# Scan: later weighing in quads of one block; convolution and token norm as one stage

## What is computed

```python
# 1. x = x + L1_conv(_gn(x)), then the layer norm of each token over its 128 channels
h = conv_depthwise_3x3(x) + dw_b
h = prune(relu(bn1(h)), 4.0)          # a channel whose maximum is under 4.0 becomes zero
h = conv_1x1(h) + pw_b
h = prune(relu(bn2(h)), 0.001)
t = to_tokens(x + h)
t = t + L2_attn(_ln_t(t), ...)        # _ln_t: (v - mean) / sqrt(var + eps) of each token

# 2. L3_attn, on 8 heads of 16 channels
iq, ik, iv = (softmax((x @ w).reshape(B, T, H, 16) / 0.1) for w in (wq, wk, wv))
a = einsum(iq, ik)                    # T x T per head
y[r, c] = a[r, c] * (y[r-1, c-1] + 1) # the scan, along each diagonal
p = causal_softmax((y + position) / 0.1)
o = einsum(p, iv)
```

## Time and profile before

| | |
|---|---|
| median of the runs | 3854.08 us (3847.75 to 3857.21) |
| the profiled execution, time / span | 3845.83 / 3844.1 us |
| TensorE clock granted, mean of the span | 0.909 of full speed |
| busy, share of the span: PE, PEld, DVE, ACT, POOL | 86%, 54%, 80%, 49%, 28% |
| convolution, from the first clearing of `pad` | 956 to 1062.4 us |
| token norm n2 | 1063.2 to 1103.6 us |
| scan of the first group: one-block quads, two-block quads | 1854 to 2156, 2156 to 2630 us |
| scan of the second group | from 2754 us, alike |

### The profile page before, as it was taken

How to read it: one execution, slowest core, us unless ns; L and a number is a source line. 1 busy time by engine, 2 the same in 40 slices (tenths; PEclk the granted TensorE clock), 3 DMA queues, 4 the chain that set the end, 5 groups by cost and what they waited for, 6 DMA issues and landing times. The chain is left out here.

```text
span 3844.1 us, 131192 instructions
## 1 busy us (share of the span) xinstructions
PE 3294.1 (86%) x53977; PEld 2075.7 (54%) x53977; DVE 3087.6 (80%) x7677; ACT 1888.9 (49%) x4422; POOL 1077.9 (28%) x1932
## 2 busy tenths in 40 slices
PE   5999999997768849966799999997689999999329
PEld 1323223332357636643577888775377788877214
DVE  7878788883868856668789999997778999997677
ACT  1666566666245524444566655553466655554200
POOL 1000111100003455520455434331165533332000
PEclk7999999999889969975799999997599999999659
DMA  7023333200010122240000000000000000000128
GB/s 151 18 41 57 57 57 57 54 8 10 0 67 27 35 57 77 78 150 18 8 10 13 12 4 9 9 6 5 7 10 10 10 10 10 10 4 6 52 95 301
DMA packets 104351, 155.92 MB, mean 41 GB/s; under 512 B 17060, under 2 KB 65193, under 8 KB 103728
## 3 DMA queue, kind: packets, MB, share of 16 engines
q1 hardware_dynamic: 90064, 121.41, 12.6%
q0 software_dynamic: 12544, 21.93, 2.1%
q10 hardware_dynamic: 1152, 4.19, 0.3%
HBM read 103.21 MB, written 45.30 MB: 39 GB/s over the span
## 5 line engine op out<-in xcount | busy, mean ns | idle before, releaser
L2095 ACT ACTIVATE s_E<-s_Y,s_M 128x9 f32<-128x9 f32 (+38 forms) x2048 | 656.6, 393 | 626.1 <-DVE s_M L2008 624.2
L369 DVE TENSOR_REDUCE half_max<-shared 128x1 f32<-128x512 f32 x1024 | 644.1, 684 | 85.7 <-PE shared L290 83.9
L1909 PE MATMUL g_x<-s_ik,s_iqm 128*32 128x1 f32 (+63 forms) x16384 | 675.2, 280 | 25.8 <-DVE g_o L1991 11.6
L492 ACT ACTIVATE E<-sc 128x1024 f32<-128x1024 f32 x512 | 497.0, 1021 | 276.1 <-PE sc L304 276.0
L2003 DVE SCALAR_TENSOR_TENSOR s_Y<-s_Y,g_x 128x9 f32<-128x9 f32 (+38 forms) x2048 | 578.2, 282 | 46.6 <-PE g_x L1909 1.2
L1921 PE MATMUL g_p<-mats,s_E 128*128 128x128 f32 x3072 | 449.9, 284 | 40.6 <-ACT s_E L2095 36.8
L1909 PEld LDWEIGHTS g_x<-s_ik,s_iqm 128*32 128x32 f32 x16384 | 393.7, 116 | 152.7 <-issue 77.1
L1921 PEld LDWEIGHTS g_p<-mats,s_E 128*128 128x128 f32 x3072 | 340.3, 144 | 107.1 <-ACT s_E L2095 62.6
L290 PE MATMUL shared<-ks,qs 96*128 96x512 bf16 x1024 | 373.6, 402 | 20.4 <-DVE half_max L369 16.7
L2008 DVE TENSOR_REDUCE s_M<-s_Y 128x4 f32<-128x8 f32 (+56 forms) x512 | 351.1, 686 | 0.2
L2019 DVE TENSOR_TENSOR resid<-g_p,s_W 128x512 f32<-128x512 f32 x384 | 263.6, 686 | 61.8 <-PE g_p L1921 58.1
(11 more groups left out here) (358 smaller groups left out, 5054.4 us busy)
## 6 DMA issues: line engine op xcount, KB each, us to landing
e_spread<-d_gate SPq DMA_DIRECT2D x64, 512.0 KB, 6.0
d_parts<-parts SPq DMA_DIRECT2D x8, 1536.0 KB, 5.9
qs<-d_parts SPq DMA_DIRECT2D x96, 128.0 KB, 7.6
ks<-d_parts SPq DMA_DIRECT2D x96, 128.0 KB, 12.4
me_xg<-d_xs SPq DMA_DIRECT2D x144, 65.0 KB, 1.8
mc_yb<-d_ys SPq DMA_DIRECT2D x8, 1024.0 KB, 5.8
resid<-in_x SPq DMA_DIRECT2D x8, 512.0 KB, 8.1
rden<-d_den POOLq DMA_DIRECT2D x16, 256.0 KB
```

What stands on the lines that cost most here:

```text
L369: dve.tensor_reduce(half_max[n // SETS % 2][:, idx // 2, idx % 2:idx % 2 + 1], bank("bm", n)[:, :], AX_X, ALU.max).then_inc(max_done, 1)
L492: act.activation(E[:, G % 2, h, :], sc[n % 2][:, :], ACT.Exp, scale=0.25).then_inc(exp_done, 1)
L1909: mm = pe.matmul(x_ps[u % 3][32 * b:32 * (b + 1), rho % 2, 0:n + 1], iqm[n // WINDOW % 2][:, b, x0:x0 + D, :], s.ik[:, b, rho, 0:n + 1], s ...
L2095: act.activation(E[:, m % 2, rho, 0:m + 1], Y[:, D * (m % YR) + rho, 1:2 + m], ACT.Exp, bias=M[:, D - 1 + D * m + rho:D + D * m + rho]).th ...
```

## The change

In the scan, a quad whose weighing has one block does it between the third and the fourth state update, where it stood between the second and the third. Quads with two blocks keep their order. In the first layers, `layer1_conv` and the call of `token_norm` for "n2" become one function, `conv_and_norm`, in one block. It makes room in PSUM by giving `c_taps`, `c_ps` and the transposed input one buffer each, where they had two, two and three. The arithmetic of both stages stays as it was.

```diff
-        taps_ps = [ctx.enter_context(nc.psum_tensor(f"c_taps{i}", [P, 2 * HALF], F32)) for i in range(2)]
-        ps = [ctx.enter_context(nc.psum_tensor(f"c_ps{i}", [P, 2 * HALF], F32)) for i in range(2)]
+        taps_ps = ctx.enter_context(nc.psum_tensor("c_taps", [P, 2 * HALF], F32))
+        ps = ctx.enter_context(nc.psum_tensor("c_ps", [P, 2 * HALF], F32))
+        turned_in = ctx.enter_context(nc.psum_tensor("c_in", [P, NT, P], F32))
+        turned_out = ctx.enter_context(nc.psum_tensor("c_out", [P, T], F32))
...
 # VectorE (moments: bn_stats, bn_aggr; norm: reciprocal, shift, four tiles)
-                for b in range(B):
-                    taps(b)
-                    if b:
-                        finish(b - 1)
-                    prune(b)
-                finish(B - 1)
+                for b in range(B + 2):
+                    if b < B:
+                        taps(b)
+                    if b >= 2:
+                        norm(b - 2)
+                    if 1 <= b <= B:
+                        finish(b - 1)
+                    if b < B:
+                        prune(b)
+                    if 1 <= b <= B:
+                        moments(b - 1)
...
 # ScalarE
+                for b in range(B + 2):
+                    if 1 <= b <= B:
                         activate(b - 1)
-                    hide(b)
+                    if b < B:
+                        hide(b)
+                    if b >= 2:
+                        scale(b - 2)
                     if b + 2 < B:
                         put(b + 2)
-                activate(B - 1)
+                    if b >= 2:
+                        store(b - 2)
+                    if 1 <= b <= B:
+                        deviation(b - 1)
...
 # TensorE
                 def taps(b):
                     pe.wait_ge(padded, b + 1)
-                    if b >= 2:
-                        pe.wait_ge(tap, TAPS * (b - 2) + 1)
+                    if b:
+                        pe.wait_ge(tap, TAPS * (b - 1) + 1)
...
                 def main(b):
                     pe.wait_ge(kept, b + 1)
-                    if b >= 2:
-                        pe.wait_ge(second_done, 2 * b - 2)
+                    if b:
+                        pe.wait_ge(second_done, 2 * b)
...
+                def turn_in(b):
+                    pe.wait_ge(added, b + 1)
+                    if b:
+                        pe.wait_ge(normed, b)
+                        pe.wait_ge(scaled, b)
...
-                for b in range(B):
-                    if b:
+                for b in range(B + 3):
+                    if b >= 3:
+                        turn_out(b - 3)
+                    if 2 <= b < B + 2:
+                        turn_in(b - 2)
+                    if 1 <= b <= B:
                         main(b - 1)
                     if b + 1 < B:
                         taps(b + 1)
-                main(B - 1)
...
 # scan_rows, VectorE
-                    if 0 <= n - 2 < QUADS:
+                    two = 0 <= n - 2 < QUADS and blocks(n - 2) == 2
+                    if two:
                         weigh(n - 2, 0)
                     if n < QUADS:
                         recur(n, 2)
-                    if 0 <= n - 2 < QUADS and blocks(n - 2) == 2:
-                        weigh(n - 2, 1)
+                    if 0 <= n - 2 < QUADS:
+                        weigh(n - 2, 1 if two else 0)
                     if n < QUADS:
                         recur(n, 3)
...
-        layer1_conv(nc, t)
         t.add_xn(nc, ctx)
-        token_norm(nc, t, "n2", "eps5")
+        conv_and_norm(nc, t)
```

More of the change, by code:

```diff
@@ L670, in taps @@
                                 dve.wait_ge(hidden_done, b - 1)
-                            before = taps_ps[b % 2][:, :].rearrange("p (y x) -> p y x", y=SIDE)
+                            before = taps_ps[:, :].rearrange("p (y x) -> p y x", y=SIDE)
                         else:
@@ L698, in prune, with moments, norm @@
                     dve.tensor_scalar(pw[b % 2][:, :], t.mat("pwT"), keep[:, 0:1], None, ALU.mult).then_inc(kept, 1)
-                for b in range(B):
-                    taps(b)
+                def moments(b):
+                    dve.wait_ge(turned, b + 1)
                     if b:
+                        dve.wait_ge(stat, 2 * b)
+                    for j in range(NT):
+                        bn = dve.bn_stats(stats[:, j, :], turned_in[:, j, :])
+                    bn.then_inc(stat, 1)
+                    dve.wait_ge(stat, 2 * b + 1)
+                    if b >= 2:
+                        dve.wait_ge(deviated, b - 1)
+                        dve.wait_ge(moved, b - 1)
+                    for j in range(NT):
+                        bn = dve.bn_aggr(mv[b % 2][:, j, :], stats[:, j, :])
+                    bn.then_inc(stat, 1)
+                def norm(b):
+                    i = b % 2
+                    dve.wait_ge(deviated, b + 1)
+                    if b >= 2:
+                        dve.wait_ge(scaled, b - 1)
+                        dve.wait_ge(back, b - 1)
+                    dve.reciprocal(rstd[i][:, :], std[i][:, :]).then_inc(recip, 1)
+                    dve.wait_ge(recip, b + 1)
+                    dve.scalar_tensor_tensor(shift[i][:, :], mv[i][:, :, 0], -1.0, rstd[i][:, :], ALU.mult, ALU.mult
+                                             ).then_inc(moved, 1)
+                    for j in range(DVE_TILES):
+                        ts = dve.tensor_scalar(xt[i][:, j, :], turned_in[:, j, :], mv[i][:, j, 0:1],
+                                               rstd[i][:, j:j + 1], ALU.subtract, ALU.mult)
+                    ts.then_inc(normed, 1)
+                for b in range(B + 2):
[4 more added lines that the diff above has]
+                    if 1 <= b <= B:
                         finish(b - 1)
-                    prune(b)
-                finish(B - 1)
+                    if b < B:
+                        prune(b)
+                    if 1 <= b <= B:
+                        moments(b - 1)
             @block.scalar
@@ L738, in _, with deviation, scale, store @@
                 act.wait_ge(folded, 9)
-                for b in range(B):
-                    if b:
+                def deviation(b):
+                    i = b % 2
+                    act.wait_ge(stat, 2 * b + 2)
+                    if b >= 2:
+                        act.wait_ge(recip, b - 1)
+                    act.activation(std[i][:, :], mv[i][:, :, 1], ACT.Sqrt, bias=t.vec("eps5")).then_inc(deviated, 1)
+                def scale(b):
+                    i = b % 2
+                    act.wait_ge(moved, b + 1)
+                    if b >= 2:
+                        act.wait_ge(back, b - 1)
+                    for j in range(DVE_TILES, NT):
+                        sc = act.activation(xt[i][:, j, :], turned_in[:, j, :], ACT.Identity,
+                                            bias=shift[i][:, j:j + 1], scale=rstd[i][:, j:j + 1])
+                    sc.then_inc(scaled, 1)
+                def store(b):
+                    act.wait_ge(back, b + 1)
+                    act.activation(t.xn[:, b * T:(b + 1) * T], turned_out[:, :], ACT.Copy).then_inc(stored, 1)
+                for b in range(B + 2):
+                    if 1 <= b <= B:
                         activate(b - 1)
-                    hide(b)
+                    if b < B:
+                        hide(b)
+                    if b >= 2:
+                        scale(b - 2)
                     if b + 2 < B:
                         put(b + 2)
-                activate(B - 1)
+                    if b >= 2:
+                        store(b - 2)
+                    if 1 <= b <= B:
+                        deviation(b - 1)
             @block.tensor
@@ L755, in taps @@
                             y0 = n // 3 + SIDE // 2 * h
[L756 removed]
+                            mmt = pe.matmul(taps_ps[:, h * HALF:(h + 1) * HALF], diag[:, k, :],
                                             pad[b % 2][:, y0:y0 + SIDE // 2, n % 3:n % 3 + SIDE],
```

29 lines of the change are left out of this document (25 added, 4 removed).

## The result

The changed kernel took 3840.82 us, the median of nine runs (3828.55 to 3845.86), and the kernel before, run beside it as often, 3854.08 us. The ratio is 0.9959, 95% interval 0.9948 to 0.997: faster by 13 us by the medians and by 16 by the ratio. The forecast was 3834.0 us and faster. The profiled execution has a span of 3839.1 us, against 3844.1.

What follows compares the result with a forecast made beforehand. VectorE was taken to bound convolution and norm, with TensorE and VectorE both near their limit in the scan's one-block quads. Scan 12 us plus convolution and norm 8 made 20, off 3854.08: 3834 us, range 3818 to 3852.

Steps and rivals of the forecast that it cites:

- The working gave 9.4 us: Convolution and norm: slots and tail added up, the merged stage ending at 1094.2 against 1103.6.
- the 8 us taken: Convolution and norm: the gain put into the sum, with ends at 3 and 10.
- The feared cost: Merged stage: if TensorE's clock stays slow, slot 1 is up to 2.7 us longer.
- the term of 12 us: Scan: later weighing in one-block quads gains 6 us a group, 12 for both, ends 0 and 20.
- the prediction's sign of being right: Scan: one-block quads done in about 296 us a group for 302.
- When the transposes are there in time nothing is won or lost: Scan: with transposes in time, swapping which two updates stand back to back was said to cost nothing.
- no worse end is reasoned: Scan: lower end is nothing, as no engine gets more work and nothing overtakes what it needs.
- TensorE's 26 waits for others: Scan: 18 waits for exponentials and 8 for state updates, at 0.28 us each 7.3 us; 6 taken.
- Rival 1: Scan: TensorE is the bound and the waits only move; only the convolution pays, 3846 us; chance 0.19.
- TensorE without pauses: Scan: rival 1's sign in the profile after, beside a shorter wait before the weighing and an equally long stretch.
- Rivals 2 and 3: Merged stage: 2, TensorE stays at 1.2 GHz, 3887, chance 0.04; 3, norm vanishes under convolution, 3801, chance 0.03.

Runs made afterwards that it cites:

- conv_only: The changed kernel with the scan's old order, so only convolution and norm are merged; 3842.84 us, ratio 0.9974.
- one_buffer: The kernel before, stages not merged, with one buffer each for `c_taps` and `c_ps`; 3853.23 us in one run.
- scan_only: The kernel before with only the scan's new order, convolution and norm not merged; 3850.47 us, ratio 1.0002.
- light_old: `conv_only` without the products with the values for rows 1 and 3 of each one-block quad; 3832.92 us in one run.
- light_new: The changed kernel without the products with the values for rows 1 and 3 of each one-block quad; 3821.06 us in one run.
- tiles_only: The changed kernel with ScalarE norming all eight tiles of images 0 to 5 and VectorE none; 3843.58 us in one run.

## Why the prediction was right, and where not

**The direction and the range held.** The time, 3840.82 us, is 6.8 us over the forecast and inside the range. Yet it held with one term of the sum nearly empty, so the parts matter more than the sum. The range was a weak test: from 3818 to 3852 us it reached to 2 us under the kernel before, and the convolution's gain alone would have lain in it. That the whole came 4 to 7 us nearer to the forecast than the parts alone add up to has no cause shown, and as far as the prediction goes it is luck.

**Convolution and norm: right, in each step.** The working gave 9.4 us, to a stage of 138.3; the trace gave 147.7 - 138.4 = 9.3, and `conv_only` 10 us as a whole kernel, with an interval of 4 us each way. In eight traces the merged stage took 137.3 to 138.6 us. The slots were 14.59 and 13.02 us, for 14.6 and 13.0. The feared cost, TensorE slow in slot 1 up to 2.7 us longer, didn't come. The pause ahead of slot 1's main product was shorter than in the old order, as in `one_buffer`. It was the old order that paid it, in the trace from which the prediction was worked out: against the 146.0 us of `scan_only` the same stage saves 7.7 us. So the 9.3 matches the working so closely because both read the same trace of before, and the 8 us taken is as good a value. The single buffers cost nothing, by `one_buffer`, and the taps of an image took 7.11 us in the 13.3 us there were. That is against the rule of the Trainium skill ("Perfetto Trace Analysis", section Optimizing Tensor Performance) only in so far as the overlap which it wants is worth nothing on an engine with time to spare.

**The scan: the term of 12 us failed.** By the traces it was about 1.3 us, and the interval of `scan_only` ends at 4. One-block quads take 302 us a group, where the prediction's sign of being right was 296. Two steps failed.

The first is "When the transposes are there in time nothing is won or lost". It compared recur 2 and recur 3 back to back with recur 1 and recur 2, as if the pairs were alike. Between the latter stands a wait for scores, and such a wait costs 0.07 us even when long met (0.39 us from start to start against 0.32). In up to 127 quads a group it is up to 8.9 us, no less than what the edit took from the waits: idle time before the updates rose by 11.4 us, where that before the weighing fell by 7.7. The statement "no worse end is reasoned" rested on the same step.

The second is that TensorE's 26 waits for others are the places where an earlier VectorE brings the transposes forward. Half of them did vanish, 5.5 us of 8.7. TensorE then stopped for "issue" instead, 7.7 us more, at the borders of its instruction packets, and its total idle time stayed at 17.4 us. The rows didn't hold the "issue" rows, of which the same view had 2.9 us, and the prediction took an engine that waits for others to be one that could go faster.

**The rivals.** Rival 1 named the outcome of the scan, "the wait before the weighing shorter but the stretch as long", though its time, 3846, lies 5 over the median. Its mechanism was half of the cause: with less work on TensorE the order was worth 8.9 us. But "TensorE without pauses", its sign, isn't what was seen: TensorE stood idle for 17.4 us, now at its own instruction borders. The other half is the wait on VectorE, which no rival had. Rivals 2 and 3 fell: in slots 1 to 6 no group of TensorE doubled its duration (in slot 7, without taps, the turning back did, behind 9.45 us), and the norm's VectorE time came on top in each slot.

**What stays open.** By their ratios the parts alone give 10.0 and -0.8 us, together 9.2, and the whole gave 15.8, in both comparisons. With half-widths of some 4.5 us on each of the three, the difference of 6.6 us is inside what they leave open together. The traces show no place where the two edits help each other.

## What to carry to other kernels

Moving an instruction changes who stands next to whom. List the waits that it carries to its new neighbour, since between two instructions of which the second reads the first, even a met wait is paid each time.

Count an engine's idle time whole, with its small gaps and with the rows that name no other engine, before a shortened wait is counted as a gain. A wait that disappears while the stretch keeps its length has moved.

Where two stages are bound by the same engine, merging them gives their ends and nothing of their middle, and the length of the merged stage can be worked out to a microsecond from the durations of one slot. The stage before has to be read from more than one trace: here one had 1.7 us that another of the same code lacked. To shorten the slot, the second engine's chain has to be moved earlier along with the work.

## What the runs showed of the hardware

A second semaphore wait on a 123-column state update that follows the one it reads cost 0.07 us, with its semaphore long set. Nothing in a list of waits shows it.

TensorE, running some 60 instructions in a microsecond in the early quads, stopped for 0.2 to 1.1 us with no semaphore to wait for. All 248 distances between such stops in eleven traces are 256 of its matmuls and weight loads or a multiple, give or take one, and 16.4 KB of instructions were loaded for every 253. Neighbouring stops lay 3.5 to 5.5 us apart, many of them 3.84. At some 50 instructions in a microsecond (`light_old`, `light_new`) the stops were nearly gone.

TensorE kept its full speed through pauses of 1.19 and 1.54 us in the merged stage (1.98 and 7.11 us for the groups behind them). Behind 4.81 us it had doubled durations (1.94 us for eight tiles, where 1.09 is usual). The pause alone doesn't decide: behind 3.85 us eight tiles took 1.07 us in the same stage. In `tiles_only` the taps behind a pause of 1.99 us took 8.80 us in one slot and 7.11 in the next. The 8.80 cost nothing, as 13.3 were free, but the slow groups behind 2.15 us in the next slot made it 16.19 us long.
